# Gated attention of a two-layer decoder: group-wise steps of four tiles replaced by walks of steps of two tiles

## The reference

```python
v = silu(xn @ v_w.T + v_b)                       # 512 wide
base = mx @ mx_w.T + mx_b
u = sigmoid(base[..., :d])
zr = silu(base[..., d:d + Z + H]); hx = base[..., d + Z + H:]
z, r = zr[..., :Z], zr[..., Z:]                  # 128 and 512 wide
z2 = z[:, :, None, :] * qk_gamma + qk_beta       # q and k
attn = softmax(q @ k.T + bias)
h = attn @ v
h = silu(hx + h * r @ h_w.T + h_b)
x4 = layernorm(x + residual + u * (h - residual))
```

## Time and profile before

| | |
|---|---|
| Median of 3 runs | 2544.44 us (2542.3 to 2545.44) |
| The profiled execution | 2543.89 us, span 2542.2 us |
| PE busy in the span | 2314.3 us (91%) |
| DVE, ACT, POOL busy | 1346.5, 1146.3, 844.6 us |
| `mega_attn` in the span | 1128.3 to 1471.5 us |

### The profile page before, as it was taken

The page is one execution under the profiler, slowest core; times in us unless marked ns, Lnnn a source line. Parts: engine busy times, 40 slices in busy tenths (PEclk is TensorE's granted clock), DMA queues, the critical chain, the costliest instruction groups (busy, mean ns, idle before and its releaser), DMA issues. The chain is left out here.

```text
span 2542.2 us, 45166 instructions
## 1 busy us (share of the span) xinstructions
PE 2314.3 (91%) x17378; PEld 1801.6 (71%) x17378; DVE 1346.5 (53%) x2520; ACT 1146.3 (45%) x1965; POOL 844.6 (33%) x873
## 2 busy tenths in 40 slices
PE   6899999799998899989889879999997799999993
PEld 5677777466665566756666658888886688888893
DVE  5688888478887581013444547788877211111113
ACT  4567676356565564533423235555654111111113
POOL 4355554244444483000010023455454122222221
PEclk9899999799999999999999989999999899999997
DMA  3534545110110569472211032333332756566564
GB/s 108 125 81 117 147 118 129 52 35 26 46 55 18 184 220 268 169 228 67 67 34 50 17 112 101 117 101 105 101 121 80 274 176 188 183 186 188 175 220 143
DMA packets 212899, 313.25 MB, mean 123 GB/s; under 512 B 63824, under 2 KB 195536, under 8 KB 199376
## 3 DMA queue, kind: packets, MB, share of 16 engines
q1 hardware_dynamic: 190832, 255.25, 31.7%
q0 software_dynamic: 13440, 17.90, 3.9%
q10 hardware_dynamic: 8416, 37.23, 3.7%
HBM read 188.88 MB, written 121.45 MB: 122 GB/s over the span
## 5 line engine op out<-in xcount | busy, mean ns | idle before, releaser
L2786 ACT ACTIVATE dec_area<-me_ps_h 128x512 f32<-128x512 f32 (+1 forms) x160 | 88.8, 555 | 424.1 <-PE me_ps_h L2764 415.3
L2827 DVE TENSOR_SCALAR me_yo<-me_ps_y,moe_xg 128x256 f32<-128x256 f32 x72 | 34.8, 483 | 429.7 <-PE me_ps_y L2774 382.3
L2702 POOL DMA_INDIRECT xo<-me_yo,me_row x72 | 112.8, 1566 | 410.9 <-DVE me_yo L2827 357.6
L2764 PE MATMUL me_ps_h<-me_xt,me_w 128*128 128x256 f32 (+1 forms) x1056 | 210.0, 357 | 0.0
L2774 PE MATMUL me_ps_y<-me_w,dec_area 128*128 128x256 f32 x944 | 209.2, 379 | 0.7 <-DVE me_yo L2827 0.7
L2237 POOL TENSOR_TENSOR l1x_e<-l1x_e,l1x_ri 128x1024 f32<-128x1024 f32 x64 | 121.8, 1903 | 239.4 <-DVE l1x_ri L2497 239.4
L2774 PEld LDWEIGHTS me_ps_y<-me_w,dec_area 128*128 128x128 f32 x944 | 178.7, 190 | 25.1 <-issue 1.1
L2764 PEld LDWEIGHTS me_ps_h<-me_xt,me_w 128*128 128x128 f32 x1056 | 181.7, 190 | 20.2
L870 POOL TENSOR_TENSOR l0x_e<-l0x_e,l0x_ri 128x1024 f32<-128x1024 f32 x64 | 120.1, 1897 | 199.3 <-DVE l0x_ri L1096 199.3
L2336 PE MATMUL l1x_ps_p<-l1x_xct,dec_area 128*128 128x256 f32 x512 | 124.8, 388 | 0.7 <-ACT l1x_xct L2422 0.7
L2374 PE MATMUL l1x_ps_o<-dec_area,l1x_ot 128*128 128x256 f32 x512 | 118.7, 385 | 1.4 <-ACT l1x_ot L2445 1.4
(11 more groups left out here) (429 smaller groups left out, 5526.4 us busy)
## 6 DMA issues: line engine op xcount, KB each, us to landing
me_w<-in_w SPq DMA_DIRECT2D x33, 2048.0 KB, 9.4
xs<-dec_zero SPq DMA_DIRECT2D x31, 1032.0 KB, 6.9
k<-kv_kt ACTq DMA_DIRECT2D x16, 1024.0 KB, 4.2
v<-kv_va ACTq DMA_DIRECT2D x16, 1024.0 KB, 5.0
l1x_kt<-k SPq DMA_DIRECT2D x16, 1024.0 KB, 5.0
l1x_va<-v SPq DMA_DIRECT2D x16, 1024.0 KB
moe_w_first<-in_w SPq DMA_DIRECT2D x7, 2048.0 KB, 9.7
moe_xg<-xs SPq DMA_DIRECT2D x32, 258.0 KB, 2.8
```

What stands on the lines that cost most here:

```text
L2702: pool.indirect_dma_start(token_rows, bass.IndirectOffsetOnAxis(row[:, j % 2, q:q + 1], 0), yo[:, j % 2, q, :], None, compute_op=ALU.add). ...
L2764: last = pe.matmul(ps_h[i % HB][:, f % 2, 0:P * size(j)], weights(j)[:, FFN * c + f * P:FFN * c + f * P + P], xt[:, j % 2, c, 0:P * size(j ...
L2786: act.activation(h[:, j % 2, 2 * i:2 * i + 2, 0:P * size(j)], ps_h[i % HB][:, :, 0:P * size(j)], ACT.Gelu).then_inc(gelued, 1)
```

## The change

The steps are cut in half: (g, 0) is tiles 0 and 1 of a group, (g, 1) tiles 2 and 3. `mix` is divided into `mix` (df, wg), `sum_mix` (res) and `moments`, each on half a group, and `root` runs once for each half. All waits stay tied to the same products, counted in halves where the product is now halved. The three orders are written as lists of (lag, step): step f runs in round n for group n - lag.

```diff
+        def walk(steps):
+            for n in range(-1, NG + 3):
+                for lag, f in steps:
+                    if 0 <= n - lag < NG:
+                        f(n - lag)
...
-                    slot_free(sp, diff_done, g, 3)
+                    slot_free(sp, diff_done, g, 3, 2)
...
-                def root(g):
+                def root(g, side):
+                    at = slice(2 * side, 2 * side + 2)
...
-                unrolled(NG, [(0, double_x), (0, spread_bias), (1, root)])
+                unrolled(NG, [(0, double_x), (0, spread_bias), (1, lambda g: root(g, 0)), (1, lambda g: root(g, 1))])
...
+                walk([(-1, lambda g: copy_xt(g, 0)), (0, lambda g: silu_v(g, 0)), (0, exponential), (0, lambda g: tanh_u(g, 0)), (0, lambda g: silu_v(g, 1)), (0, lambda g: silu_r(g, 0)), (-1, lambda g: copy_xt(g, 1)), (0, copy_et), (1, lambda g: silu_h(g, 0)), (0, lambda g: silu_r(g, 1)), (1, lambda g: silu_h(g, 1)), (-1, silu_z), (0, lambda g: tanh_u(g, 1))])
...
-                def mix(g):
+                def mix(g, side):
+                    at = slice(2 * side, 2 * side + 2)
+                    item_done(dve, h_done, 2 * g + side)
                     item_done(dve, x_loaded[g % 3], g // 3, 16 * G)
-                    slot_free(dve, mixed, g, 1)
-                    dve.tensor_tensor(df[:, :, :], ho[:, :, :], x[:, g % 3, :, :], ALU.subtract).then_inc(diff_done, 1)
+                    slot_free(dve, mixed, 2 * g + side, 2)
+                    dve.tensor_tensor(df[:, at, :], ho[:, at, :], x[:, g % 3, at, :], ALU.subtract).then_inc(diff_done, 1)
...
+                def sum_mix(g, side):
...
+                def moments(g, side):
...
+                walk([(0, lambda g: bias_u(g, 0)), (0, scale_z), (0, lambda g: bias_v(g, 0)), (0, lambda g: bias_u(g, 1)), (0, shift), (0, lambda g: bias_v(g, 1)), (1, lambda g: bias_h(g, 0)), (0, scale_e), (0, lambda g: gate(g, 0)), (2, lambda g: apply(g, 0)), (0, lambda g: gate(g, 1)), (2, lambda g: apply(g, 1)), (1, lambda g: mix(g, 0)), (1, lambda g: sum_mix(g, 0)), (1, lambda g: bias_h(g, 1)), (1, lambda g: moments(g, 0)), (1, lambda g: mix(g, 1)), (1, lambda g: sum_mix(g, 1)), (1, lambda g: moments(g, 1))])
...
                 def project_z(g):
+                    if g == 0:
+                        pe.wait_ge(spread_done, 1)
+                        pe.matmul(ps_s[:, 0, :], rt[:, 0, :], rt[:, 1, :], start=True, stop=True).then_inc(bias_mm, 1)
+                        pe.wait_ge(w_loaded, W_LOADS)
...
                 def score(g):
+                    if g == 0:
+                        pe.wait_ge(bm_done, 1)
...
+                walk([(0, lambda g: project_u(g, 0)), (0, project_z), (0, lambda g: project_v(g, 0)), (-1, lambda g: transposes(g, 0)), (0, lambda g: project_u(g, 1)), (0, score), (0, lambda g: project_v(g, 1)), (1, lambda g: project_h(g, 0)), (-1, lambda g: transposes(g, 1)), (0, lambda g: project_r(g, 0)), (0, transpose_e), (0, lambda g: project_r(g, 1)), (0, lambda g: attend(g, 0)), (0, lambda g: attend(g, 1)), (1, lambda g: project_h(g, 1))])
```

More of the change, by code:

```diff
@@ L1813, in silu_z, with silu_v @@
                     act.activation(z[:, :], ps_z[:, :], ACT.Silu, bias=zp[:, 0:1]).then_inc(z_done, 1)
-                def silu_v(g):
-                    for t in range(G):
+                def silu_v(g, side):
+                    for t in (2 * side, 2 * side + 1):
                         item_done(act, v_biased, G * g + t)
@@ L1839, in copy_et, with silu_h @@
                     act.activation(et[:, :, :], ps_s[:, :, :], ACT.Copy).then_inc(et_copied, 1)
[L1841 to L1844, removed]
+                def silu_h(g, j):
+                    item_done(act, h_biased, 2 * g + j)
+                    act.activation(ho[:, 2 * j:2 * j + 2, :], ho[:, 2 * j:2 * j + 2, :], ACT.Silu).then_inc(h_done, 1)
                 act.wait_ge(w_loaded, W_LOADS)
[L1846 to L1859, removed]
+                walk([(-1, lambda g: copy_xt(g, 0)), (0, lambda g: silu_v(g, 0)), (0, exponential), (0, lambda g: tanh_u(g, 0)), (0, lambda g: silu_v(g, 1)), (0, lambda g: silu_r(g, 0)), (-1, lambda g: copy_xt(g, 1)), (0, copy_et), (1, lambda g: silu_h(g, 0)), (0, lambda g: silu_r(g, 1)), (1, lambda g: silu_h(g, 1)), (-1, silu_z), (0, lambda g: tanh_u(g, 1))])
                 act.wait_ge(bv_multiplied, 1)
@@ L1990, in _, with transposes @@
             @block.tensor
             def _(pe):
-                def transposes(g):
-                    for i in range(4):
+                def transposes(g, side):
+                    for i in (2 * side, 2 * side + 1):
                         c = 1 - i // 2
@@ L2010, in project_z, with project_v @@
                     last.then_inc(z_projected, 1)
-                def project_v(g):
+                def project_v(g, side):
                     pe.wait_ge(xt_copied, 4 * g + 4)
-                    for t in range(G):
+                    for t in (2 * side, 2 * side + 1):
                         if t >= 2:
@@ L2029, in score, with project_r @@
                     last.then_inc(scored, 1)
-                def project_r(g):
-                    for c in range(4):
+                def project_r(g, side):
+                    for c in (2 * side, 2 * side + 1):
                         if c >= 2:
@@ L2040, in project_r, with project_u @@
                         last.then_inc(r_projected, 1)
-                def project_u(g):
-                    for t in range(G):
+                def project_u(g, side):
+                    for t in (2 * side, 2 * side + 1):
                         if t % 2 == 0:
@@ L2056, in transpose_e, with project_h @@
                     last.then_inc(e_transposed, 1)
[L2058 removed]
+                def project_h(g, side):
                     item_done(pe, gated, g, G)
[L2060 removed]
+                    for t in (2 * side, 2 * side + 1):
                         if t % 2 == 0 and g + 1 < NG:
```

125 lines of the change are left out of this document (42 added, 83 removed).

## The result

The changed kernel takes 2500.32 us (2497.95 to 2505.26, four runs) against 2544.94 us (2542.3 to 2547.42, four runs) for the one before: ratio 0.9823, 95% interval 0.9808 to 0.9838; the forecast was 2505.2, with a range of 2500 to 2516. In the profiled execution, of 2499.9 us, the span fell from 2542.2 to 2497.7 us, by 44.5. Of these, 38.5 lie in `mega_attn`, for which 39.2 were forecast (1128.30 to 1471.54 before, 1122.22 to 1426.94 now). The code ahead of the stage is the same in both kernels but took 6.1 us less this time, and what follows took the same within 0.1 us (1070.7 and 1070.8).

What follows compares the result with a forecast made beforehand. PE's work plus waits from its neighbours' orders was taken to bound the stage. Gains of 4.5, 2.0, 24.4, 5.5 and 2.8 us make 39.2, off the 2544.4 median: 2505.2 us; own range 2502 to 2510, wider range 2500 to 2516.

Steps and rivals of the forecast that it cites:

- Both waits: PE's idle time in a round: 2.48 us at project_v from DVE's order, 1.24 at project_r from ACT's table loads.
- round 0: First round of mega_attn: PE's work of 26.0 us from 1131.8 ends at 1157.8, not 1162.3, a gain of 4.5 us.
- rounds 2 to 6: The full rounds of mega_attn: five times 4.88 us less, a gain of 24.4 us.
- rounds 7 and 8: Last rounds of mega_attn, together 50.3 us before: 36.15 without 1.76 for transposes, plus 10.4, a gain of 5.5 us.
- the end: From the last bias_h to the end of apply: 7.2 us with halves instead of 10.0, a gain of 2.8 us.
- The clock is up by then: PE in the stage's first round: its work from 1131.8 was priced as if the clock had already risen.
- POOL beside DVE: root(·,0) beside mix(·,1): cost between 0 and 1.6 us, nothing in rounds, 0 to 1.4 at the stage's end; taken as 0.
- The slacks: Time inputs lie ready before PE's steps: score 2.7 us, project_v(g,1) 2.9, attend for copy_et 1.2, transposes for loads 4.5.
- (a): Rival: one wait a round survives, 1.24 to 2.48 us in 7 rounds, 9 to 17 us: 2514 to 2522; chance 0.15.
- (b): Rival: the waits only move, and all 5 us of each round come back: 2540 to 2549; chance 0.03.
- (c): Rival: the loop from project_h over DVE to score becomes the bound, slower than before at 15.1 us; chance 0.04.
- the gain is kept: Rest of the program: nothing after the stage has a date of its own to wait for, so the 39.2 us stay.

## What of the prediction held, and which step failed

**Bound and mechanism: right.** PE's work without waits was put at 35.9 to 36.15 us a round, and it is 36.24. Both waits had the causes named: the kernel with `mix` moved alone takes away the one and leaves the other. The terms of the sum, in us:

| Term | forecast | measured | second pair |
|---|---|---|---|
| round 0 | 4.5 | 33.98 - 30.83 = 3.15 | 4.5 |
| round 1 | 2.0 | 38.18 - 36.21 = 2.0 | 2.0 |
| rounds 2 to 6 | 24.4 | 205.20 - 181.19 = 24.0 | 25.7 |
| rounds 7 and 8 | 5.5 | 50.31 - 44.85 = 5.5 | 5.5 |
| the end | 2.8 | 15.57 - 11.64 = 3.9 | 3.9 |
| the stage together | 39.2 | 38.5 | 41.6 |
| outside the stage | 0 | 6.0 | -4.6 |

(After the change round 0 is counted to the start of `project_u(1,0)`, with which a round begins now, 1.73 us ahead of `project_z(1)`: 32.56 - 1.73 = 30.83. The same 1.73 go to rounds 7 and 8: 43.12 + 1.73 = 44.85. The second pair is the traces of both kernels run again; its 25.7 holds the 1.7 us that the clock took from before in round 2.)

**Round 0 was over by 1.35.** "The clock is up by then" failed. The first steps of PE in the stage:

```profile
1122.26 3.87 PE L1984 MATMUL ma_ps_t<-dec_ident,mw_xin 128*128 128x128 f32 x16 [5.33 <-PEq L85]
1125.92 2.95 PE L2035 MATMUL ma_ps_u<-mw_w_uh,cv_t 128*128 128x256 f32 x8
...
1128.93 1.88 PE L1995 MATMUL ma_ps_z<-cv_t,mw_w_z 128*128 128x512 f32 x4
```

After the barrier's 5.33 us of standing the clock was still low during `project_u`, which the new order puts first: it took 2.8 us (1125.92 to 1128.71, where the two small matmuls ahead of `project_z` start) instead of 1.73. In the first trace of before, on which the sum was made, the clock was up 3.3 us after the stage's start, ahead of every 512-wide matmul; here it rose after 5.8. Over the twelve traces it rose between 3.3 and 6.3 us after the start. In the second pair, where it rose after 6.2 and 5.4 us, round 0 gave the forecast 4.5 us. So the term was taken from one favourable execution of before.

**The end was under by 1.1.** Its chain from `bias_h` to the end of `apply` is 7.0 us (1415.57 to 1422.56), forecast 7.2. What I left out is that from there to the next stage pass 4.4 us instead of 5.3. It was so in both traces of the changed kernel and of before. The last `apply` now covers two tiles instead of four, so that the first two of its group's stores can go out before it; that this is the reason was not tried.

**POOL beside DVE.** I took 0 for it, and the end's 7.0 bears that out for the change's own time; the 1.4 us that the prediction had worked out from the Trainium skill were not lost. But the sharing exists. The rows first: POOL's root is 0.59 and 1.16 beside `mix` and 0.20 and 0.73 away from it, with DVE at its 0.69 each time; six additions of DVE and POOL's `double_x` are both longer (5.86 for 4.29, 2.44 for 1.89); and the keys' instruction took 2.23 us beside a `double_x` in round 2:

```profile
1195.04 2.23 DVE L1885 TENSOR_SCALAR ma_kt<-ma_z,mw_zp 128x512 f32<-128x512 f32 x1
1195.10 1.89 POOL L1790 TENSOR_TENSOR cv_xg<-cv_xg 128x1024 f32<-128x1024 f32 x1
```

This agrees with the Trainium skill (SBUF — State Buffer, Who interferes with whom), by which whoever has the shared port pair keeps it for its whole instruction. POOL then waits for one instruction of DVE, at most 0.7 us here, and DVE for one of POOL, which for `double_x` is 1.89. The prediction had reckoned that POOL's small instructions would hold up the chain; the chain went on, and POOL's waited, beside slack. The larger case it overlooked: the same section of the Trainium skill also names `tensor_scalar` among those that can contend, so `scale_z` and a long `double_x` were the pair to look at. It takes 1.7 us of the slack in rounds 2 and 7 and nothing of the time. In round 7, which the prediction did not look at by itself, the slack is 2.2 without it, and with it 0.5 are left (the keys are ready at 1378.56, score starts at 1379.06).

**ACT and the slacks.** ACT was busy 13.43 us a round, not 14.2: pairs of activations now follow each other without a gap and overlap (silu_v takes 1.15 for two tiles, where one took 0.63). DVE was busy 0.3 us a round more (19.5 for 19.2), not 0.5 to 1. The slacks looked up in round 6 were right within 0.6, and each on the low side: 3.07 for 2.7, 3.4 for 2.9, 1.5 for 1.2, and 4.6 to 5.1 for the loads' 4.5. None of the rivals (a), (b) or (c) came about. For (c) the additions give the measured price: the loop may be 3.07 us longer, beyond that each us costs one, and at a stand of 2.62 us another 1.8 through the clock, so that the gain is all but gone at six additions, 5.9 us, and not at the 8.4 that I had worked out from waits alone (15.1 - 6.7).

**How the numbers follow.** The step that failed is the term for the rest of the program, which the prediction put at nothing. It made its sum against one profiled execution, took it over to the median, and reasoned that nothing after the stage has a date of its own, "so the gain is kept"; of the code ahead of the stage it said nothing. So "2502 to 2510" and then "2500 to 2516" held the bounds of the stage's terms alone. In the first pair of traces the code ahead of the stage took 6.1 us less, more than the 4.9 by which the time lies under the forecast, while the stage gave 0.7 less than its 39.2. The result lies under the first range and at the low end of the second; as a ratio, 0.9823 of the 2544.44 from which the prediction started is 2499.4, below both. That this code moves from execution to execution, by 13 us in twelve traces, is shown; why it does stays open, and the other three executions of the first result have no trace. Two medians of the same changed kernel are 2500.3 and 2508.3, one on either side of 2505.2, so it is partly luck which of them a forecast meets. No term of the stage's sum was off by more than 1.4. Three us more on both sides would have been honest.

## What to carry to other kernels

Where an engine is busy nine tenths of a stage and its waits come from its neighbours' orders, lay its own steps on a line at their start distances, look up for each when its input is there, and order the neighbours so that every one has 1 to 3 us to spare; here the sum then held within a tenth of a microsecond a round. Put an activation whose input is ready by then behind a table change, so that the load does not stand before one that is waited for. Compare the stretches of two traces one by one before you credit a difference to a change: here 1.0 of 1.2 us came from the clock at the stage's start. Count the spread of the unchanged part into the range, and a stand of the matrix engine of 2.5 us as 0 to 1.8 us more than its length.

## What the runs showed of the hardware that I had not expected

- The clock's fall in mid-stream: after PE stood 2.49 and 2.62 us, 0.50 (1.2 GHz) was granted for about 3 us, and the next 8 matmuls of 512 columns took 5.40 us instead of 3.70 and 5.00 instead of 3.60. With six additions it happened after the stands of 2.61 and 2.62 in rounds 3 to 6 (40.79 to 40.81) and after the 3.48 of round 7, and not after the 2.51 of round 2; of the stands of 2.48 to 2.57 in the two traces of before it followed one; after 0.64 to 1.60 the clock stayed at 1.00.
- A DVE instruction of 0.54 us taking 2.11 to 2.24 beside one of POOL of 1.9 us, when POOL's began from 0.16 us ahead of it to 0.06 behind. With the loads later it did so in each of rounds 2 to 7. Where POOL's began 0.12 and 0.19 us behind it, DVE's took its 0.54 and POOL's 2.18 and 2.11.
- The clock's rise after a barrier, on the same code ahead: between 3.3 and 6.3 us after the stage's start, worth 1.1 us of the stage in the order of before (35.10 and 33.99 us to `project_z(1)`) and up to 1.3 in the changed one (32.80 and 31.48).
- ACT's table load of 1.28 us comes ahead of the wait in one place (1.75 us before the exponential's input) and behind it in another (2.63 us of idle time, then the load). What decides between the two was not tried.
